# Last recurrence of a four-layer kernel: adding the states in DRAM by an accumulating transfer instead of on VectorE

## The reference

```python
def _L3_cond_ref(h_t, z, W, b, alpha):
    Wh, Wz = W[:, :D], W[:, D:]
    leak = 1.0 - alpha
    def step(h, z_t):
        gate = jax.nn.sigmoid(h @ Wh.T + z_t @ Wz.T + b)
        h_new = jnp.tanh(h * leak + gate * z_t)
        return (h_new, h_new)
    _, hs = jax.lax.scan(step, h_t, jnp.swapaxes(z, 0, 1))
    return jnp.swapaxes(hs, 0, 1)
...
x = x + _L3_cond_ref(cond_1024, x, L3_cond_W, L3_cond_b, L3_cond_alpha)
```

## Time and profile before

| What | Value |
|---|---|
| Device time, median of 3 runs | 1973.86 us (1972.1 to 1974.81) |
| Span of the profiled execution | 1969.9 us |
| Device time of the profiled execution itself | not recorded apart |
| Mean granted TensorE clock | 0.997 |
| Busy share: PE, DVE, ACT, POOL | 98%, 57%, 42%, 7% |
| The last recurrence | from 1686 us to the end |

### The profile page before, as it was taken

One profiled execution on the slowest core, in us unless ns is written; L12 is line 12 of the kernel. 1 busy time (PEld: TensorE's weight loads), 2 busy tenths in 40 slices (PEclk: granted clock), 3 DMA queues, 4 the chain that ended last, 5 costly groups with the idle time before them and its releaser, 6 DMA issues. The chain is left out here.

```text
span 1969.9 us, 45643 instructions
## 1 busy us (share of the span) xinstructions
PE 1937.0 (98%) x18112; PEld 1152.3 (58%) x18112; DVE 1116.9 (57%) x2453; ACT 822.9 (42%) x1701; POOL 141.5 (7%) x144
## 2 busy tenths in 40 slices
PE   8999989999999999999999999999999999999997
PEld 6999954444444444444444444444455555899996
DVE  5666656644896645111111137555655674789997
ACT  4444445422121434343333345322333332577775
POOL 0000000000000000221121111111110110000000
PEclk9999999999999999999999999999999999999999
DMA  7033347764342423999998955533322335100111
GB/s 302 14 134 134 128 139 225 198 176 139 109 174 103 171 93 106 242 217 212 220 211 202 187 195 160 172 104 92 83 75 91 102 86 188 45 3 34 50 46 46
DMA packets 281898, 266.31 MB, mean 135 GB/s; under 512 B 225991, under 2 KB 233293, under 8 KB 275086
## 3 DMA queue, kind: packets, MB, share of 16 engines
q1 hardware_dynamic: 270942, 228.73, 40.2%
q0 software_dynamic: 10800, 35.40, 6.9%
HBM read 153.70 MB, written 56.36 MB: 107 GB/s over the span
## 5 line engine op out<-in xcount | busy, mean ns | idle before, releaser
L1111 PE MATMUL sh_p<-xh,arena 128*128 128x512 f16 x2048 | 610.5, 380 | 2.6 <-PEq L1798 1.6
L1111 PE MATMUL sh_p<-xl,arena 128*128 128x512 f16 x1024 | 388.6, 380 | 0.0
L1111 PEld LDWEIGHTS sh_p<-xh,arena 128*128 128x128 f16 x2048 | 200.5, 98 | 245.2 <-issue 4.0
L1126 PE MATMUL p<-sh_h_hi,arena 128*128 128x512 f16 x1024 | 304.6, 379 | 0.0
L1286 ACT CAST sh_h_hi<-sh_half_h 128x512 f16<-128x512 f32 x128 | 79.0, 617 | 348.6 <-DVE sh_half_h L1661 348.6
L1909 DVE SCALAR_TENSOR_TENSOR ro_hs<-ro_h,fac,ro_hs 128x512 f16<-128x512 f32 x71 | 53.4, 752 | 300.8 <-ACT ro_hs L1895 271.1
L1280 ACT ACTIVATE sh_sig<-sh_p,fac 128x512 f32<-128x512 f32 x128 | 87.9, 686 | 268.1 <-PE sh_p L1111 267.9
L1852 PE MATMUL ro_py<-arena,ro_ht 128*128 x852 | 195.3, 379 | 3.0 <-DMA ro_ht<-ro_hs 3.0
L1126 PE MATMUL p<-sh_h_lo,arena 128*128 128x512 f16 x512 | 194.0, 379 | 0.0
L1658 DVE SCALAR_TENSOR_TENSOR sh_half_h<-sh_sig,sh_p 128x512 f32<-128x512 f32 x128 | 87.6, 684 | 148.7 <-ACT sh_sig L1280 145.7
L1111 PEld LDWEIGHTS sh_p<-xl,arena 128*128 128x128 f16 x1024 | 100.4, 98 | 121.3 <-issue 0.8
(11 more groups left out here) (287 smaller groups left out, 3213.0 us busy)
## 6 DMA issues: line engine op xcount, KB each, us to landing
stage<-in_shared_w SPq DMA_DIRECT2D x29, 768.0 KB, 5.2
routed_rows<-xres SPq DMA_DIRECT2D x71, 256.0 KB
stage<-in_norms_r SPq DMA_DIRECT2D x16, 1024.0 KB, 4.8
stage<-in_routed_w SPq DMA_DIRECT2D x16, 1024.0 KB, 4.8
stage<-in_norms SPq DMA_DIRECT2D x14, 1024.0 KB, 5.0
arena<-x SPq DMA_DIRECT2D x12, 1024.0 KB, 5.9
rnn_xs<-in_x SPq DMA_DIRECT2D x8, 1024.0 KB, 19.6
x<-xres SPq DMA_DIRECT2D x16, 512.0 KB, 2.6
```

The source lines that it names most:

```text
L1111: mm = nc.tensor.matmul(p1[u % P1][:], arena[:, w:w + P], x[slot(gl)][:, :, k, :], start=(j == 0), stop=(j == 3 * KD - 1))
L1126: mm = nc.tensor.matmul(p2[m][:], arena[:, w:w + P], h[n % 2][:], start=(i == 0 and j == 0), stop=(i == HID - 1 and j == 2))
```

## The change

At the start of the last recurrence SP copies each chunk of `x3` to the same place in the output, DRAM to DRAM: 16 transfers of 512 KB that wait for nothing (`copy_across`). POOL now takes part in the full round: it waits for all 16 copies, and then for each chunk waits until the previous chunk's addition has landed, tells ACT so (`hist_free`), waits until the chunk's states are complete (`h32_ready`), and issues a transfer from `hist[p]` to the output with `accum_op=ALU.add`. DVE no longer adds, and `xo` isn't used in this layer. ACT waits on `hist_free` where it waited on `summed`. The first recurrence (the one with `gate`) stays as it was.

```diff
+        copied, adding, hist_free = sem("copied"), sem("adding"), sem("hist_free")
...
-                sp.sem_inc(summed, 2)
+                sp.sem_inc(summed if gate else hist_free, 2)
...
+                def copy_across(q, p, c, o, u, ahead):
+                    rows = [t[bass.ds(c, 1)].rearrange("o p k n -> p (o k) n") for t in (x_out, x_in)]
+                    sp.dma_start(*rows).then_inc(copied, 16)
...
-                    full_chunks(sp, r, store)
+                    full_chunks(sp, r, store if gate else copy_across)
...
+                def add_states(q, p, c, o, u, ahead):
+                    if not (isinstance(o, int) and o == 0):
+                        wait_alone(pool, stored[1 - p], (u + p) * 16, 16)
+                        pool.sem_inc(hist_free, 1)
+                    wait_alone(pool, h32_ready, (q * CHUNK_STEPS + CHUNK_STEPS + 1) * parts, parts)
+                    pool.sem_inc(adding, 1)
+                    pool.dma_start(x_out[bass.ds(c, 1)].rearrange("o p k n -> p (o k) n"), hist[p][:], accum_op=ALU.add).then_inc(stored[p], 16)
+
+                def full_round(r):
+                    wait_alone(pool, copied, r * CHUNKS * 16, CHUNKS * 16)
+                    full_chunks(pool, r, add_states)
...
                         if j == 0 and o is not None:
-                            act.wait_ge(summed, o + 1)
+                            act.wait_ge(summed if gate else hist_free, o + 1)
...
-                        if o is not None:
+                        if o is not None and gate:
                             if j == 0:
                                 wait_alone(dve, stored[p], (u + 1) * 16, 16)
                             add = nc.vector.tensor_tensor(xo[p][:, :, cols], xs_chunk(c)[:, :, cols], hist[p][:, :, cols], ALU.add)
```

More of the change, by code:

```diff
@@ L148, in over_rounds @@
                     further_rounds()
-                    ready["further"][eng.engine]()
+                    if eng.engine in ready["further"]:
+                        ready["further"][eng.engine]()
                 nc.switch_bb(over)
@@ L182, in _ @@
                 sp.sem_inc(hd_ready, parts)
-                for s in stored:
-                    sp.sem_inc(s, 16)
-                sp.sem_inc(summed, 2)
+                if gate:
+                    for s in stored:
+                        sp.sem_inc(s, 16)
+                sp.sem_inc(summed if gate else hist_free, 2)
                 if gate:
@@ L224, in full_round @@
                             sp.wait_ge(raw_in[i], 16 * (1 + (CHUNKS - 4) // 2))
-                    if leaky or not isinstance(r, int):
+                    if leaky:
+                        for p in range(2):
+                            wait_alone(sp, stored[p], r * (CHUNKS // 2) * 16, 16)
+                    elif not isinstance(r, int):
                         for p in range(2):
@@ L235, in _ @@
                     nc.gpsimd.memset(h_hi[:], 0.0).then_inc(zeroed, 1)
+                    return
+                def add_states(q, p, c, o, u, ahead):
[8 more added lines that the diff above has]
+                    full_chunks(pool, r, add_states)
+                over_rounds(pool, lambda: None, full_round)
             @block.tensor
```

## The result

| | Before | After |
|---|---|---|
| Device time, median (lowest to highest, 9 runs each) | 1973.58 us (1971.81 to 1974.81) | 1977.97 us (1976.27 to 1981.86) |
| Ratio after to before, 95% interval | | 1.0024 (1.0016 to 1.0032) |
| Span of the profiled execution | 1969.9 us | 1981.0 us |

The change makes the kernel slower, by 4.4 us (0.2%) between the medians. The forecast was 1970.2 us, with 1974.7 us as the upper end.

The account below looks back on a forecast made before the run. The prediction took DVE to lead the loop by 0.12 us a step, with PE next. Copies costing nothing, -5.9 us for the loop and +2.2 at the end gave -3.7 us: 1970.2 us, range 1966.5 to 1974.7.

Parts of the forecast that it names:

- The copies: Warm-up of the last recurrence: SP's 16 copies (8.4 MB) take no instructions or operands from PE and cost nothing.
- The loop: Full round: without DVE's additions, 12 chunks fall from 11.97 to 11.47 us, chunk 13 gives 0.15; taken as 5.9 us.
- the loop is not freed: Rival: something else, such as PE's branch each pass, keeps chunks near 11.97 us; gain 0 to 3 us; chance 0.08.
- The end: End of round: the last adding transfer lands later than the old store, making the end 2.2 us later.
- L: Time from issue to landing of POOL's adding transfer: taken as 7.0 us, within an estimate of 5.5 to 7.6.
- quick landing: Rival, end of round: the adding transfer lands after 2.7 to 5.5 us; total change -8.0 to -5.2 us; chance 0.18.
- The charge for the addition: POOL's adding transfer: reading 512 KB of its destination adds 2.1 us, if not overlapped, on a gather-based estimate.
- The rule of the Trainium skill: GpSimd-issued transfers: 2.0 us plus bytes at 436 GB/s, so the addition lands after 3.2 us; sum -7.5 us.
- During the round: Full round: additions landing within 11.5 us stay hidden behind PE's chunk, and ACT never waits for POOL.
- The sum: Whole kernel: copies nothing, loop -5.9 us, end +2.2 us, together -3.7 us.

Follow-up runs that it names:

- e2: The changed kernel with each copy waiting for the warm-up to advance one and a half steps: 1973.36 us, ratio 1.0003 to the kernel before.
- e3: The changed kernel without the copies and without POOL's wait for them: 1972.76 us, ratio 0.9999 to the kernel before.
- e9: The changed kernel without POOL's adding transfers, its 16 copies sent to an unused tensor in mid-loop of the full round: 1972.25 us, ratio 0.9987.
- e10: The changed kernel without adding transfers, its copies sent to an unused tensor mid-round, the full round's loop written out: 1972.94 us, ratio 0.9995.
- e7: The kernel before, additions kept on DVE, with the last recurrence's full-round loop written out: 1967.41 us, ratio 0.9971.
- e4: The changed kernel without copies, POOL's transfers storing the states instead of adding them: 1973.72 us, ratio 0.9999 to the kernel before.
- e8: The changed kernel, its 16 copies sent instead to an unused tensor in mid-loop of the full round, adding transfers kept: 1980.06 us, ratio 1.0032.
- e5_unrolled: The changed kernel, copies as they are, with the last recurrence's full-round loop written out: 1975.75 us, ratio 1.0016 to the kernel before.

## Why the prediction was wrong

- **The copies: the step that failed.** "So traffic of this kind doesn't take PE's instructions or operands from it ... They cost nothing." The row behind it had 212 GB/s in a stretch of the experts, and was taken for a worst case. The engines were as busy there (0.98), but the traffic was of another kind: 83187 of its 90819 packets were under 512 B, and its code drew 10 packets of instructions (q8) in 200 us, where the warm-up drew 13 in 80. The copies ran at 346 GB/s, 100% of the DMA engines' time, in rows of 32 KB (16 x 8192 elements in the listing), during code that is written out and must be brought in. Which of the two differences spared the experts wasn't tested. PE waited 5.4 us and then ran at the lower clock: +7.3 us in the first profile, +3.8 in the second, in place of 0. Pacing or leaving out the copies removes all of it (e2, e3), and the pair e9 and e10 tells instructions from traffic. The prediction put the copies at nothing also because SP had nothing else to do; but SP isn't the only user of the DMA engines. The Trainium skill says (DMA: Bandwidth & Descriptors, section Queues, rings and completion order) that each DMA engine takes turns between its queues packet by packet; the rows with 32 KB and with 4 KB, 3.8 to 7.3 against 1.9 to 2.4 us of warm-up lost, go the way that this rule would have them. That the wait is a turn behind a long row is inferred from that, not shown, and the timed runs of the small rows don't bear it out.
- **The loop: right that DVE led, wrong about what stood next.** "The difference between warm-up and loop is the addition of L636" left out the sequencers' register instructions, which the listing of a loop step shows and which `wait_alone` adds only where a semaphore's value depends on the loop's counter. The gain was 1.87 us in place of 5.9. With the addition gone, the chain is the bound in three steps of four: 0.11 us more from sigmoid to tanh than in the warm-up, 2.91 us a step. The first step of a chunk stays at 3.08 us, where PE waits for `x_lo`. That step also opens chunk 13, whose 11.62 us are the same after the change: the 0.15 us that the prediction took from it were not the addition's either. The rival "the loop is not freed" named this with 0.08 and a branch as its cause; the loss is in every step instead, and writing out the loop removes it. e7 shows the other half: without the loop the addition is hidden, and costs 0.03 us a chunk.
- **The end: mechanism right in part, size off.** L was 5.3 us in the median and 5.7 for the last transfer, not 7.0, and POOL took 0.56 us from the tanh to the issue where 0.1 was charged: 6.3 us against 7.1 from tanh to landing. The term is +0.6 us in place of +2.2. "Which changes the end by L - 4.8 us" holds only for slow landings: e4 and e9 show that the end gains at most 0.7 us by a quick one, so the rival "quick landing", priced at up to -2.1 us there, couldn't have paid that. The charge for the addition was good (2.1 forecast, 2.3 to 2.4 measured by e4); the base was bad, since a gather (4.4 us) isn't the nearest thing to a direct store by POOL (2.9 us). The rule of the Trainium skill quoted in the prediction gives 3.2 us: it is near the plain store and 2.1 us below the adding one.
- **During the round: right.** The additions land well inside a chunk and ACT never waits for them; e8 shows the price when two are late (13.2 and 15.2 us, a chunk of 18.63).
- **The sum.** Forecast 0 - 5.9 + 2.2 = -3.7 us; the first profile gives 7.3 - 1.9 + 0.6 = +6.0, the second 3.8 - 1.8 + 0.5 = +2.5, the timed runs +4.4. Without the copies' loss (e2 and e3, 1973.4 and 1972.8 us) the time would have been 2.6 to 3.2 us above the forecast and inside its range.

Open: why the smaller rows, with 2 us of loss in the warm-up in both profiles, are as slow as the changed kernel in timed runs. Their layer (277.8 and 277.2 us) would put them about 1 us above the kernel before, and they are 3.6 above. Part of it may lie ahead of the layer, where these profiles alone differ by 3.7 us (1695.23 and 1698.97); stalls may also be longer in the executions without a profile. Neither was measured.

## What to carry to other kernels

Instructions come in through the same 16 DMA engines as data (the rows of the queues above give the share of both), and a dense burst of copies beside new code stalled PE here. Before a large transfer is put beside code that is written out, compare it with a stretch that the trace shows without a stall, in the length of its rows and in how much new code runs there, not only in how busy the engines are; and pace it if nothing needs it soon. If a loop runs slower than the same work written out, look at the sequencer's instructions between the engines' work before removing work: here writing out six passes gave more than taking 64 additions away.

## What the runs showed of the hardware

- 16 copies of 512 KB from DRAM to DRAM with rows of 32 KB ran at 346 GB/s as the profile counts them.
- An adding transfer of 512 KB from SBUF to DRAM lands 5.3 us after POOL issues it (5.0 to 5.7), a plain one 2.9 us, and two beside 8.4 MB of other traffic 13.2 and 15.2 us.
- Behind a wait of 2.38 us PE was granted a clock of 0.57 over 4 us (the changed kernel), behind one of 2.00 us 0.83 over 10 us (`e10_burst_new_code`); behind its waits of 1.47 and 1.55 us, and behind one of 2.10 us in `e5_unrolled`, it stayed at 1.00. So the length of the wait alone doesn't say whether the clock falls. This is `e5_unrolled` right behind that wait:

```profile
1720.03:1724.00 3.97, 3.97 (x88) 3.77 (x88) 2.69 (x10) 2.77 (x9) 0.00 (x0) 1.00 0.68 211
```
